# Scaling the decay triangle on ScalarE in four 128x128 copies per head pair, with a new order of steps

## The reference

```python
q = silu(conv4(x @ Wq)); k = silu(conv4(x @ Wk)); v = silu(conv4(x @ Wv))
gk = -exp(A_log) * softplus(x @ Wgk + dt_bias); beta = sigmoid(x @ Wb + b_b)
S = S * exp(gt)
delta = (vt - einsum('bhk,bhkv->bhv', kt, S)) * bt
S = S + einsum('bhk,bhv->bhkv', kt, delta)
ot = einsum('bhk,bhkv->bhv', qt, S)
```

## Time and profile before

| what | us |
|---|---|
| runs | 3057.14, 3064.13, 3064.31; median 3064.13 |
| profiled execution | 3054.66 |
| its span, first to last instruction | 3052.9 |
| TensorE busy | 2657.3 |
| VectorE busy | 2522.1 |
| ScalarE busy | 2201.2 |
| GpSimd busy | 1625.6 |

### The profile page before, as it was taken

One profiled execution on the slowest core, in us unless ns is written; L12 is line 12 of the kernel. 1 busy time (PEld: TensorE's weight loads), 2 busy tenths in 40 slices (PEclk: granted clock), 3 DMA queues, 4 the chain that ended last, 5 costly groups with the idle time before them and its releaser, 6 DMA issues.

```text
span 3052.9 us, 83158 instructions
## 1 busy us (share of the span) xinstructions
PE 2657.3 (87%) x25361; PEld 2131.6 (70%) x25487; DVE 2522.1 (83%) x7140; ACT 2201.2 (72%) x6626; POOL 1625.6 (53%) x2418
## 2 busy tenths in 40 slices
PE   4789898889888898988989889899888988889986
PEld 3577777777767677776777667777677776767775
DVE  7888898888788887888878888888888888888872
ACT  3677777777677777776767767777777777777774
POOL 3565554565544556445654446554456654456651
PEclk8899999999999999999999989999999999999997
DMA  2111011111011111111110111101111101111101
GB/s 64 22 34 35 15 33 35 35 24 35 16 34 35 24 35 25 24 35 24 35 36 14 35 29 30 36 16 34 36 27 32 35 16 34 35 24 35 33 16 23
DMA packets 319431, 91.35 MB, mean 30 GB/s; under 512 B 283057, under 2 KB 310001, under 8 KB 318961
## 3 DMA queue, kind: packets, MB, share of 16 engines
q1 hardware_dynamic: 318960, 85.59, 13.5%
HBM read 46.76 MB, written 38.80 MB: 28 GB/s over the span
## 4 chain that ended last, share of the span: by engine, by line
PE 54%; DVE 25%; issue 11%; ACT 4%; POOL 3%; DMA 1%; DVEq 1%; SPq 0%; ACTq 0%; POOLq 0%
DVE KQ L914 6%; PE ring L1382 5%; PE ring L1228 5%; DVE UP L1010 5%; PE bank_o L1349 4%; PE ring L1211 4%; PE ring L1178 3%; PE ring L1169 3%; PE bank_e L1318 3%; PE bank_e L1331 3%; PE bank_e L1335 2%; PE ring L1241 2%; DVE ssr L979 2%; PE bank_o L1355 2%; PE bank_e L1326 2%
## 5 line engine op out<-in xcount | busy, mean ns | idle before, releaser
L614 POOL TENSOR_TENSOR laneA<-laneA,laneT 96x30 f32<-96x30 f32 (+14 forms) x960 | 520.3, 542 | 75.3
L611 POOL TENSOR_TENSOR laneT<-laneA 96x30 f32<-96x30 f32 (+14 forms) x960 | 498.9, 520 | 68.0
L914 DVE SCALAR_TENSOR_TENSOR KQ<-ring,ckq,KQ 128x255 f32<-128x255 f32 (+2 forms) x1152 | 460.5, 476 | 17.5 <-DVE nabs L949 6.5
L914 DVE SCALAR_TENSOR_TENSOR vc<-ring,cvv,vc 128x255 f32<-128x255 f32 (+2 forms) x1152 | 462.8, 476 | 3.9 <-ACT vc L718 0.8
L598 POOL TENSOR_TENSOR sqk<-sse,phalf 128x8 f32<-128x8 f32 x96 | 157.4, 1639 | 576.9 <-DVE sse L984 576.9
L1010 DVE SCALAR_TENSOR_TENSOR UP<-ring,cj,gm 128x256 f32<-128x256 f32 x768 | 327.2, 478 | 26.7 <-PE ring L1195 14.9
L1055 DVE SCALAR_TENSOR_TENSOR V<-bank_o,negG,V 128x128 f32<-128x128 f32 x384 | 134.3, 350 | 202.9 <-PE bank_o L1355 146.3
L592 POOL TENSOR_TENSOR gm<-g,mle 128x512 f32<-128x512 f32 x192 | 197.6, 1051 | 179.0 <-DVE UP L1010 165.9
L1211 PE MATMUL ring<-xnT,wv 128*128 128x256 f32 x768 | 231.8, 430 | 62.7 <-DVE KQ L914 53.9
L1169 PE MATMUL ring<-gm,mgt 128*128 128x512 f32 x384 | 218.7, 654 | 59.1 <-DVE UP L1010 58.3
L1178 PE MATMUL ring<-xnT,wqk 128*128 128x256 f32 x768 | 237.2, 446 | 36.6 <-issue 34.5
(11 more groups left out here) (164 smaller groups left out, 7902.6 us busy)
## 6 DMA issues: line engine op xcount, KB each, us to landing
to_lanes<-UP SPq DMA_DIRECT2D x128, 96.0 KB, 2.7
laneA<-to_lanes SPq DMA_DIRECT2D x32, 384.0 KB, 3.5
from_lanes<-laneA SPq DMA_DIRECT2D x32, 384.0 KB, 3.0
UP<-from_lanes SPq DMA_DIRECT2D x128, 96.0 KB, 3.0
turned_lanes<-laneX SPq DMA_DIRECT2D x32, 288.0 KB
N<-turned_lanes SPq DMA_DIRECT2D x96, 96.0 KB, 2.7
xin<-_attn_hidden_states_dram SPq DMA_DIRECT2D x32, 128.0 KB, 2.7
xres<-_attn_hidden_states_dram SPq DMA_DIRECT2D x32, 128.0 KB, 3.2
```

Source lines behind the costliest of these rows:

```text
L611: link(nc.gpsimd.tensor_tensor(t, A[:, 0:m, j:j + 1].broadcast_to([LANES, m, n]), A[:, j:j + 1, j + 1:BLK].broadcast_to([LANES, m, n]), AL ...
L614: link(nc.gpsimd.tensor_tensor(w, w, t, ALU.add))
L914: ins = nc.vector.scalar_tensor_tensor(acc[:, n, s:T], src[:, n * T:n * T + T - s], wt(n)[:, TAPS - 1 - s:TAPS - s], acc[:, n, s:T], ALU.m ...
```

## The change

The product of DDg is taken from GpSimd. ScalarE does it in four copies of 128x128 for a head pair, each with the rates of one head and chunk as its per-partition scale. The waits are the same: for g, and for the GRr steps that last read the buffer. A wait is added to XN, for the product GP 5 of two iterations before, which reads the xnT buffer that XN overwrites. All of `ORDER` is written anew, with the same 272 steps; TSTORE, VPs 4 and VPs 5 have another offset, since they now stand at the end of the iteration before. Shown of it are the old lines around the last GRr, the new lines from the start to beyond the last GRr, and the last new lines.

```diff
 ORDER = (
...
-    ("XQ0", 1, 1), ("MY2r", 1, 0), ("QTr", 5, 1), ("QN", 4, 1), ("DDr", 4, 1), ("GRr", 5, 1), ("QN", 5, 1),
-    ("SE", 4, 0), ("GR", 3, 1), ("GR", 4, 1), ("MZ", 2, 0), ("GRr", 6, 1), ("MZr", 2, 0), ("SO", 5, 0),
-    ("SE", 5, 0), ("DD", 5, 1), ("SSr", 2, 1), ("GRr", 7, 1), ("MX", 2, 0), ("DDr", 5, 1), ("CJ", 2, 1),
-    ("GRr", 8, 1), ("VPs", 0, 1), ("SO", 6, 0), ("GRr", 9, 1), ("MZ2r", 1, 0), ("SE", 6, 0), ("GR", 5, 1),
-    ("GRr", 10, 1), ("SE", 7, 0), ("GRr", 11, 1), ("SO", 7, 0), ("MY2r", 2, 0), ("XQ", 0, 1), ("VP", 3, 1),
-    ("VPr", 3, 1), ("LOUT", 0, 1), ("XQr", 0, 1), ("SO", 8, 0), ("SE", 8, 0), ("FU", 0, 1), ("LN2", 0, 2),
...
+    ("QK", 0, 1), ("ZB", 0, 1), ("VT", 3, 0), ("ZBr", 0, 1), ("QKr", 0, 1), ("VP", 0, 1), ("ZBe", 0, 1),
+    ("QK", 1, 1), ("QKr", 1, 1), ("VP", 1, 1), ("STORE", 0, 0), ("VTr", 3, 0), ("VPr", 0, 1), ("QKt", 0, 1),
+    ("QK", 2, 1), ("QK", 3, 1), ("ZBg", 0, 1), ("VPr", 1, 1), ("GC", 0, 1), ("QKr", 2, 1), ("QKr", 3, 1),
+    ("QKt", 1, 1), ("TFETCH", 0, 0), ("DDg", 0, 1), ("FETCH", 0, 0), ("GCr", 0, 1), ("QKs", 0, 1),
+    ("QKs", 1, 1), ("QKt", 2, 1), ("VT", 2, 0), ("VPt", 1, 1), ("QK", 4, 1), ("QKs", 2, 1), ("VTr", 2, 0),
+    ("DDg", 1, 1), ("VT", 5, 0), ("VT", 4, 0), ("QKr", 4, 1), ("QT", 0, 1), ("QKt", 3, 1), ("VTr", 5, 0),
+    ("VP", 2, 1), ("QTr", 0, 1), ("QT", 1, 1), ("VTr", 4, 0), ("QKs", 3, 1), ("VPr", 2, 1), ("DD", 0, 1),
+    ("QTr", 1, 1), ("QKt", 4, 1), ("VPt", 2, 1), ("DDg", 2, 1), ("QT", 2, 1), ("DDr", 0, 1), ("QK", 5, 1),
+    ("QKr", 5, 1), ("DD", 1, 1), ("DD", 2, 1), ("QTr", 2, 1), ("DDr", 1, 1), ("QN", 0, 1), ("MY", 0, 0),
+    ("MYr", 0, 0), ("MY", 1, 0), ("QN", 1, 1), ("QT", 3, 1), ("MZ", 0, 0), ("VPt", 0, 1), ("SSr", 0, 1),
+    ("DDg", 3, 1), ("DDr", 2, 1), ("MYr", 1, 0), ("DD", 3, 1), ("MZ", 1, 0), ("QKt", 5, 1), ("MZr", 0, 0),
+    ("QN", 2, 1), ("GR", 0, 1), ("QTr", 3, 1), ("DDr", 3, 1), ("CJ", 0, 1), ("QN", 3, 1), ("MZr", 1, 0),
+    ("GRr", 0, 1), ("GRr", 1, 1), ("GR", 1, 1), ("GRr", 2, 1), ("GR", 2, 1), ("MY2", 0, 0), ("QKs", 4, 1),
+    ("DDg", 4, 1), ("GRr", 3, 1), ("QT", 4, 1), ("DD", 4, 1), ("SSr", 1, 1), ("MY", 2, 0), ("MY2r", 0, 0),
+    ("CJ", 1, 1), ("DDg", 5, 1), ("GRr", 4, 1), ("GRr", 5, 1), ("QKs", 5, 1), ("XQ0", 0, 1), ("QTr", 4, 1),
+    ("MYr", 2, 0), ("DDr", 4, 1), ("GR", 3, 1), ("MX", 1, 0), ("MZ2r", 0, 0), ("DD", 5, 1), ("SE", 3, 0),
+    ("XQ0", 1, 1), ("XQ", 0, 1), ("QN", 4, 1), ("MY2r", 1, 0), ("QT", 5, 1), ("QTr", 5, 1), ("GRr", 6, 1),
+    ("GRr", 7, 1), ("QN", 5, 1), ("SE", 4, 0), ("MZ", 2, 0), ("SSr", 2, 1), ("GR", 4, 1), ("DDr", 5, 1),
+    ("CJ", 2, 1), ("GRr", 8, 1), ("MZr", 2, 0), ("GR", 5, 1), ("SE", 5, 0), ("GRr", 9, 1), ("VPs", 0, 1),
+    ("XR", 0, 0), ("XQr", 0, 1), ("GRr", 10, 1), ("SO", 5, 0), ("MX", 2, 0), ("GRr", 11, 1), ("SE", 6, 0),
...
+    ("GPr", 4, 0), ("OG", 3, 0), ("OT", 3, 0), ("LANEP", 5, 1), ("KTr", 1, 1), ("LANEP", 6, 1), ("OTr", 2, 0),
+    ("WO", 1, 0), ("VPs", 3, 1), ("LANEP", 7, 1), ("OG", 4, 0), ("VP", 5, 1), ("GPr", 5, 0), ("OTr", 3, 0),
+    ("WO", 2, 0), ("OG", 5, 0), ("VPr", 5, 1), ("XN", 0, 2), ("XNr", 0, 2), ("OT", 4, 0), ("VT", 1, 1),
+    ("WO", 3, 0), ("TSTORE", 0, 1), ("OT", 5, 0), ("HT", 1, 1), ("OTr", 4, 0), ("OTr", 5, 0), ("HTr", 1, 1),
+    ("VPt", 5, 1), ("WO", 4, 0), ("WO", 5, 0), ("VPs", 4, 1), ("VPs", 5, 1), ("VTr", 1, 1), ("YOr", 0, 0),
 )
```

```diff
@@ -580,18 +580,6 @@
                         pool.wait_ge(s_var, cnt(i, 1, 1))
                         nc.gpsimd.tensor_tensor(out=rstd[:, :], in0=veps[:, :], in1=mhalf[:, 0:NT],
                                                 op=ALU.pow).then_inc(s_rstd, 1)
-                    if kind == "DDg":
-
-                        if a == 0:
-                            pool.wait_ge(s_g, cnt(i, 1, 1))
-                        p, back = (a - 4, 0) if a >= 4 else (a + 2, 1)
-                        if not back or not zero(i):
-
-                            pool.wait_ge(read("GR", p, 0), rv(i - back, "GR", p, 0))
-                            pool.wait_ge(read("GR", p, 1), rv(i - back, "GR", p, 1))
-                        nc.gpsimd.tensor_tensor(out=decay(a), in0=bc(g[:, :, 2 * a:2 * a + 2].rearrange("p t h -> p h t"), 3, P),
-                                                in1=mle[:, :].unsqueeze(1).unsqueeze(1).broadcast_to([P, 2, NT, P]),
-                                                op=ALU.mult).then_inc(s_gm, 1)
                     if kind == "CJ":
                         pool.wait_ge(s_sse, cnt(i, NG, a + 1))
                         uq = slice(GH * a, GH * a + GH)
@@ -673,6 +661,10 @@
                     elif kind in RING:
                         continue
                     if kind == "XN":
+                        if not early(i):
+
+                            split(act, full("XN", 0), full("GP", 5))
+                            act.wait_ge(full("GP", 5), rv(i - 2, "GP", 5))
                         nc.scalar.activation(xnT[:, par(), :], b[:, 0:T], ACT.Copy).then_inc(read("XN", 0), 1)
                     if kind == "ZBe":
                         act.wait_ge(s_z, cnt(i, 1, 1))
@@ -684,6 +676,19 @@
                     if kind == "GC":
                         nc.scalar.activation(eG2[:, par(), :], b[:, 0:NU], ACT.Exp)
                         nc.scalar.activation(eR[:, :], b[:, NU:2 * NU], ACT.Exp).then_inc(read("GC", 0), 1)
+                    if kind == "DDg":
+
+                        if a == 0:
+                            act.wait_ge(s_g, cnt(i, 1, 1))
+                        p, back = (a - 4, 0) if a >= 4 else (a + 2, 1)
+                        if not back or not zero(i):
+
+                            act.wait_ge(read("GR", p, 0), rv(i - back, "GR", p, 0))
+                            act.wait_ge(read("GR", p, 1), rv(i - back, "GR", p, 1))
+                        for n in range(2 * NT):
+                            h, t = 2 * a + n // NT, n % NT
+                            ins = nc.scalar.activation(decay(a)[:, n // NT, t, :], mle[:, :], ACT.Copy, scale=g[:, t, h:h + 1])
+                        ins.then_inc(s_gm, 1)
                     if kind == "DD":
 
                         nc.scalar.activation(decay(a).rearrange("p h t n -> p (h t n)"), b[:, :], ACT.Exp)\
```

More of the change, by code:

```diff
@@ L53 @@
 ORDER = (
[L54 to L67, removed]
[10 rows of a table removed]
-    ("GP", 0, 0), ("MZ2r", 2, 0), ("SQ", 11, 0), ("LANEP", 0, 1), ("FUm", 1, 1), ("VPs", 1, 1), ("LANEP", 1, 1),
[12 rows of a table removed]
@@ L91 @@
-    ("HT", 1, 1), ("OTr", 4, 0), ("VT", 1, 1), ("LANEP", 6, 1), ("HTr", 1, 1), ("OTr", 5, 0), ("XNr", 0, 2),
-    ("VTr", 0, 1), ("VTr", 1, 1), ("WO", 4, 0), ("WO", 5, 0), ("LANEP", 7, 1), ("YOr", 0, 0),
+    ("QK", 0, 1), ("ZB", 0, 1), ("VT", 3, 0), ("ZBr", 0, 1), ("QKr", 0, 1), ("VP", 0, 1), ("ZBe", 0, 1),
+    ("QK", 1, 1), ("QKr", 1, 1), ("VP", 1, 1), ("STORE", 0, 0), ("VTr", 3, 0), ("VPr", 0, 1), ("QKt", 0, 1),
+    ("QK", 2, 1), ("QK", 3, 1), ("ZBg", 0, 1), ("VPr", 1, 1), ("GC", 0, 1), ("QKr", 2, 1), ("QKr", 3, 1),
@@ new lines @@
+    ("DDg", 4, 1), ("GRr", 3, 1), ("QT", 4, 1), ("DD", 4, 1), ("SSr", 1, 1), ("MY", 2, 0), ("MY2r", 0, 0),
+    ("CJ", 1, 1), ("DDg", 5, 1), ("GRr", 4, 1), ("GRr", 5, 1), ("QKs", 5, 1), ("XQ0", 0, 1), ("QTr", 4, 1),
[3 rows of a table added]
+    ("CJ", 2, 1), ("GRr", 8, 1), ("MZr", 2, 0), ("GR", 5, 1), ("SE", 5, 0), ("GRr", 9, 1), ("VPs", 0, 1),
[3 rows of a table added]
+    ("FUr", 0, 1), ("FUr", 1, 1), ("LLOAD", 0, 1), ("FUm", 0, 1), ("FUm", 1, 1), ("SQ", 8, 0), ("VPs", 1, 1),
[11 rows of a table added]
+    ("GPr", 4, 0), ("OG", 3, 0), ("OT", 3, 0), ("LANEP", 5, 1), ("KTr", 1, 1), ("LANEP", 6, 1), ("OTr", 2, 0),
```

## The result

| | median us | lowest to highest | ratio to before on the same chip, 95% interval |
|---|---|---|---|
| before | 3064.22 | 3057.14 to 3066.81 | |
| changed | 3024.17 | 3013.99 to 3025.13 | 0.9865, 0.9839 to 0.9892 |

The change takes 40 us off, 1.35%, where 18 were forecast.

What follows compares the result with a forecast made beforehand. The prediction took VectorE to bound the front (to the last GRr's end) and TensorE the back. Terms -26 + 12 - 4 = -18 us gave a median of 3046; own range 3025 to 3055, 8 in 10 from 2985 to 3112.

Steps and rivals of the forecast that it cites:

- gm leaves GpSimd: Taking gm off hidden GpSimd gains nothing itself, but frees VectorE's cj and bq ahead of GRr 4: -26 us.
- the hold: GpSimd's gm product locks the shared port, delaying VectorE's cj (21.8 us) and bq (4.4): together 26 us.
- the order: Steps moved between front and back: VectorE's front -1.92 us, TensorE's back +1.78 an iteration, -4 us in all.
- gm arrives on ScalarE: 24 copies of 286 ns add 6.9 us an iteration to ScalarE, mostly covered: +12 us exposed, ends 0 and 213.
- The premise: Ahead of the last GRr's end VectorE bounds (92% busy), behind it TensorE; VectorE savings count only ahead.
- the order does more: Rival: TensorE's idle time in the back absorbs the moved work, the front's 2.7 us gain stays whole: 2991, chance 0.12.
- The ScalarE term: Exposed cost of the gm copies on ScalarE, taken from its share of the chain: 213 / 18 = +12 us.
- one part in 18: Exposed share of ScalarE's copies, from its 4% of the chain at 72% busy: 12 of 213 us.
- The slower rival: ScalarE becomes the front's bound, with DDg 4 and 5 copies exposed, 2.3 us an iteration: 3106, chance 0.33.
- Queues and waits at 0: TSTORE's new place on SP, TFETCH's landing before MY (slack 1.1 us) and XN's added wait cost 0.

Runs made afterwards that it cites:

- gm5_behind_cj: The kernel before with one step moved by one place: DDg 5 behind CJ 1, gm still on GpSimd; 3009.11 us, ratio 0.9815.
- order_only: The kernel before with the new ORDER and the wait added to XN, gm still on GpSimd; 3009.86 us, ratio 0.9825.
- gm5_ahead_in_new: order_only with DDg 5 put ahead of CJ 1 again, so that the hold returns; 3036.23 us, ratio 0.9934.
- gr4_twice: The kernel before with the products of GR 4 issued twice, ahead of TensorE's idle stretch before DD 5; 3029.47 us, ratio 0.9906.
- copies_of_64: The changed kernel with each ScalarE copy of 128x128 cut in two of 128x64; 3114.38 us, ratio 1.0161 to before.
- engine_only: The changed kernel with the old ORDER, gm in copies on ScalarE; 3129.82 us, ratio 1.0211 to before.
- late_gm_scalar_old: The kernel before, old list, with XN's added wait and gm of pairs 4 and 5 on ScalarE, 0 to 3 on GpSimd; 3017.62 us, ratio 0.9870.
- late_gm_on_pool: The changed kernel with gm of pairs 4 and 5 on GpSimd again, 0 to 3 on ScalarE; 3017.11 us, ratio 0.9868 to before.
- order_again: order_only repeated unaltered on the same chip as changed_again; 3013.00 us, ratio 0.9862 to before.
- changed_again: The changed kernel repeated unaltered on the same chip as order_again; 3026.19 us, ratio 0.9896 to before.

## Why the prediction was right and wrong, point by point

**The sum.** By steps, from the medians of the runs (each a difference of two kernels, good to some 5 to 10 us) and, for the two parts of the first term, from the traces:

| term | forecast | measured | from |
|---|---|---|---|
| gm leaves GpSimd | -26, ends 0 and -35 | -58 | before to gm5_behind_cj |
| of it the hold | -26 | -25, in the new list -20 to -33 | before to gm5_behind_cj, second cj to front's end; order_only to gm5_ahead_in_new |
| of it the clock | none | -17 | the same stretch, before to gm5_behind_cj and to gr4_twice |
| the order | -4 | +1 | gm5_behind_cj to order_only |
| gm arrives on ScalarE | +12 | +14, +13 | order_only to changed, twice |
| sum | -18 | -43 | measured whole: -40 |

**The step that failed** is the size of the first term, "gm leaves GpSimd". Its working was (394 - 167) x 96 and (218 - 172) x 96: the length of the hold, once. That part was right: 25 us in the traces. It left out what TensorE does while it waits, and that took 17 more. The prediction listed what is late behind cj (GRr 4, and so the front's end), but not DD 5, whose bank wait grows by the same 0.84 us, and it has no term for the granted clock, 0.93 in the front. The low end of -35 was drawn from other small steps of VectorE, which had nothing to do with it. A list of the low stretches by place in the iteration, which the trace of before would have given, shows 17 behind a held cj.

What this rests on: gr4_twice takes the low clock away with the hold left in, gm5_ahead_in_new puts the hold in where no low stretch comes of it, and in the trace of before the iterations with and without the low clock stand side by side. The two parts come to 42 us, where gm5_behind_cj is 47 faster by the profiled executions and 58 by the medians. Before's median lies between 3056.40 and 3067.87 in the three batches of experiments, and its profiled execution at 3054.66; the 11 us between 47 and 58 are not explained. For the same reason not all of the miss from -18 to -40 has a cause here: 10.5 us of it are in no trace. Between the profiled executions the change is -29.5, and there the clock's 17 us are more than the whole miss of 11.5; the order (+3 and not -4) and the copies (+15 and not +12) go the other way.

**The premise** "the front is VectorE's and the back is TensorE's, and a microsecond off VectorE counts only in the front" is wrong in its last part. It did not hurt the sum, for a reason that it did not know: the order's two halves are -1.93 us in the front and +1.90 in the back (gm5_behind_cj to order_only in the table), as forecast (-1.92, +1.78), but LN alone, without a product moved, lengthens the back by 1.45 us. The forecast had the back grow by TensorE's products, so that its two halves came out is luck. The rival "the order does more" (2991) was built on the premise that moved work vanishes in TensorE's idle time; it does not.

**The ScalarE term** has the right size by a working that does not hold, which is luck. The share of one part in 18, from the chain, would make copies_of_64's 133 us of work cost 7; they cost 88. What makes 246 us of copies cost only 13 is the new list, and beyond them the margin is used up. Where in it the copies find room was not taken apart. In the old list they cost 121 (gm5_behind_cj's 3009 to engine_only's 3130, neither with a hold). So the order, near 0 by itself in forecast and measurement once no cj is held, is what makes the engine change bearable.

**The slower rival** (3106, ScalarE as the front's bound) is real as a mechanism: engine_only is it, and lies 2.1% above before. Its place, DDg 4 and 5 behind their GRr waits, was wrong for the old list: late_gm_scalar_old puts exactly these on ScalarE and gains 39 us, and the exposed groups are the early ones. In the new list the place was right and the price too high: there the stretch behind the second cj is 0.2 to 0.3 us an iteration longer with the copies, and not 2.3, and late_gm_on_pool, without those of pairs 4 and 5, has none of it.

**Queues and waits at 0** held. Of the terms put at nothing, the wait of the MY products for the DMA of TFETCH shows once in the changed kernel, at the first sequence, and XN's added wait not at all; the largest wait for an SP transfer is GpSimd's own:

```profile
POOL laneA L594 <- DMA laneA<-to_lanes: 197.9, 32, 10.6
PE ring L1264 <- DMA N<-turned_lanes: 16.6, 1, 16.6
```

**The numbers.** 3024.17 is inside the range of 8 in 10 and 1 us outside the forecast's own, 3025 to 3055, on its fast side.

**The better version.** gm5_behind_cj, with gm on GpSimd as before and one step moved by one place, took 3009.11 us: 1.85% off, where the change takes 1.35. order_only stands level with it. The gain of this change comes from gm 5 not running beside cj, for which no engine had to be changed; the change of engine gives some 13 us of it back.

**Open.** What sets the other low stretches is not known. Those that begin 9 to 25 us into an iteration last 187.7 us in before, 221.9 in order_only and 256.0 in the changed kernel, but in the second pair 242.3 (order_again) and 238.9 (changed_again), where the copies cost as much. So these stretches differ from execution to execution, and no run says what they cost. The runs of before lie between 3033 and 3073 us over the three chips and may differ in them.

## What to carry to other kernels

When an operation takes longer beside one of another engine, look first whether one of the two can be moved by a place in the order; changing the engine costs the new engine's time as well. Price a stall that ends in TensorE's wait with its own length and with what the granted clock does behind it: list the low stretches by place in the iteration, and see what idle time stands ahead of each. And a share of the chain is no price for added work: double the work once, or find where in the iteration the engine is full.
